# Attention of a post-norm block rebuilt: transposed projections, two-piece scores, heads in row halves

## Chip, cores and metric

One core of a Trainium2 chip runs the program. The metric is device time in microseconds (us) of one execution. The kernel before takes 1507.37 us, median of 3 runs (1506.63 to 1508.64).

## What is computed

The change touches the first third of one layer: attention over 8 sequences of 512 rows, width 256, 16 heads of 16. What follows it (first layer norm, router, shared and routed experts, second norm) is the same in both kernels.

```python
def _L0_attn_ref(x, Wqkv, Wo):            # x (8, 512, 256), H = 16, DH = 16
    qkv = (x @ Wqkv).reshape(b, l, 3, H, DH)
    q, k, v = (qkv[:, :, 0], qkv[:, :, 1], qkv[:, :, 2])
    q = q * cos + rotate_half(q) * sin
    k = k * cos + rotate_half(k) * sin
    scores = jnp.einsum('bqhd,bkhd->bhqk', q, k) * DH ** (-0.5)
    attn = jax.nn.softmax(scores, axis=-1)
    out = jnp.einsum('bhqk,bkhd->bqhd', attn, v).reshape(b, l, d)
    return out @ Wo
x = _layernorm(x + _L0_attn_ref(x, L0_attn_Wqkv, L0_attn_Wo), axis=-1)
```

## The kernel before

`attention` works in 32 groups (NG), each of four heads of one sequence. A group has 16 units (U): one unit is one head against one tile of 128 rows. Every engine runs the same hand-written order, `period(p)`, whose step u names what is issued there; semaphores join the engines. For p from -6 to 0 the pipeline fills, a loop runs three passes of eight periods, and the rest is unrolled.

In step u of period p TensorE (PE) issues `score_cols` (L271 to L279: keys by queries into one of two banks psB) for the group p, and `score_rows` (L261 to L269: queries by keys into one of three banks psA) 20 units ahead. VectorE (DVE) takes the row maxima of psA (`row_max`, L470). The maxima are split into three bf16 pieces (`split_max`), turned by 16 small transposes (`turn_max`, L316) and copied into rows 96 to 98 of the query operand, where the column scores subtract them. ScalarE (ACT) takes the exponent of psB (`exps`, L387) into a ring of eight tiles; `add_pv` (L329), once every four steps, multiplies four of them by V in four column strips of the array. ACT copies the sum out (`copy_out`, L399), PE turns it (`turn_out`, L337), DVE divides by the sum of the exponents (`norm_out`, L500 and L510).

Before a head can be scored, q and k are projected row tile by row tile (`project`, L350 to L352, 3 matmuls in fp32r for each half of the width), rotated on DVE (`rope`, L526 to L530) and POOL (L245), split into three bf16 pieces by DVE and POOL in turns (L538, L247, L543, L249, L251), spread over six terms on ACT (`spread`, L414 to L417), turned by 8 transposes a head (`turn_head`, L293) and copied to SBUF (`copy_head`, L394). V is projected in step 12. Each x tile is split by ACT (`x_hi`, L424) and POOL (`x_lo`, L236). SyncE (SP) only loads x, stores the output (L200, L203), zeroes the slot buffer at the start (L191, ten stores) and loads the attention rows back (L595).

## Time and profile before

| | |
|---|---|
| time, median of 3 | 1507.37 us |
| profiled execution: time, span | 1512.29 us, 1510.5 us |
| granted TensorE clock, mean | 0.929 |
| busy: PE, DVE, ACT, POOL | 87%, 69%, 65%, 34% of the span |
| longest group: row maxima, L470 | 512 times, 338.9 us |
| second: exponents, L387 | 512 times, 290.0 us |

A busy share is that of the whole span, so it averages the attention with the expert stages behind it. A row "x512 | 338.9, 682" is a count, the total busy time in us and the mean of one in ns. A row of the timeline begins with the start and the duration, both in us; matmuls are pipelined, so the step from one start to the next is their cost, not the duration. What stands in square brackets or behind the last bar is idle time of the engine and what ended it.

### The profile page before, as it was taken

The numbers are of one execution on the slowest core, as the hardware profiler recorded it, in microseconds if no ns is written. First come the engines' busy times: TensorE is split into PE (matmuls) and PEld (weight loads), VectorE is DVE, ScalarE is ACT, GpSimd is POOL, SyncE is SP. The second block draws the span as 40 slices with busy tenths as digits, with TensorE's granted clock in tenths as the row PEclk, the third lists the DMA queues.
The fourth block names the chain that finished last, engine by engine and source line by source line (L and its number), as shares of the span: only waits on it lengthen the run. The fifth ranks groups of instructions, "written<-read, shape, count | busy, mean of one in ns | idle before, by whom it ended". The sixth has DMA issues, their size and how long they took to land. (4 is left out here: it accounts for less than half of the span.)

```text
span 1510.5 us, 30476 instructions
## 1 busy us (share of the span) xinstructions
PE 1317.0 (87%) x9849; PEld 1007.7 (67%) x9920; DVE 1044.7 (69%) x2129; ACT 979.6 (65%) x2014; POOL 518.4 (34%) x493
## 2 busy tenths in 40 slices
PE   3899999999999999689802989999999999997585
PEld 2544444444444443378702989999999999997485
DVE  3788877887888878387401557777777777775377
ACT  5588878887888888477301437666666666664265
POOL 6222212121222200064574004444444444445542
PEclk7799999999999999998955998999999999998698
DMA  8000010001000003320321006677777667762333
GB/s 335 1 1 29 2 31 1 30 1 31 2 29 2 15 1 112 123 74 18 109 104 70 0 19 233 221 221 237 238 231 239 220 219 236 235 217 63 101 102 95
DMA packets 113899, 160.46 MB, mean 106 GB/s; under 512 B 12928, under 2 KB 95872, under 8 KB 112640
## 3 DMA queue, kind: packets, MB, share of 16 engines
q1 hardware_dynamic: 107648, 142.32, 28.5%
q0 software_dynamic: 6144, 16.79, 3.5%
q8 instruction: 58, 0.95, 0.3%
q14 instruction: 49, 0.40, 0.1%
HBM read 121.86 MB, written 37.22 MB: 105 GB/s over the span
## 5 line engine op out<-in xcount | busy, mean ns | idle before, releaser
L470 DVE TENSOR_REDUCE att_mx<-att_psA 128x1 f32<-128x512 f32 x512 | 338.9, 682 | 62.0 <-PE att_psA L269 59.7
L387 ACT ACTIVATE att_prob<-att_psB 128x512 f32<-128x512 f32 x512 | 290.0, 602 | 81.4 <-PE att_psB L279 69.9
L1465 ACT ACTIVATE exp_psU<-exp_psU,ew_b 128x256 f32<-128x256 f32 x312 | 126.8, 444 | 154.2 <-PE exp_psU L1422 154.2
L269 PE MATMUL att_psA<-att_qk 96*128 96x512 bf16 x512 | 197.8, 388 | 8.9 <-DVE att_mx L470 5.3
L1497 DVE CAST exp_hh<-exp_psU 128x512 fp32r<-128x512 f32 x156 | 107.4, 688 | 110.2 <-ACT exp_psU L1465 110.2
L1420 PE MATMUL exp_psU<-exp_xh,exp_w1h 128*128 128x256 f32 x624 | 177.9, 285 | 2.1 <-DVE exp_w1l L1492 2.1
L1405 PE MATMUL exp_psD<-exp_w2h,exp_hh 128*128 128x256 f32 x624 | 179.6, 288 | 0.0
L1422 PE MATMUL exp_psU<-exp_xh,exp_w1l 128*128 128x256 f32 x624 | 177.5, 285 | 0.0
L1421 PE MATMUL exp_psU<-exp_xl,exp_w1h 128*128 128x256 f32 x624 | 177.5, 284 | 0.0
L279 PE MATMUL att_psB<-att_qk 128*128 128x512 bf16 x441 | 170.2, 387 | 7.8 <-issue 5.3
L1407 PE MATMUL exp_psD<-exp_w2h,exp_hl 128*128 128x256 f32 x624 | 176.5, 283 | 0.0
L1406 PE MATMUL exp_psD<-exp_w2l,exp_hh 128*128 128x256 f32 x624 | 176.5, 283 | 0.0
L1373 POOL TENSOR_TENSOR exp_w2l<-ew_w,exp_w2h 128x512 fp32r<-128x512 f32 x80 | 105.3, 1316 | 139.9 <-ACT exp_w2h L1456 139.9
L1373 POOL TENSOR_TENSOR exp_w2l<-exp_w,exp_w2h 128x512 fp32r<-128x512 f32 x76 | 100.0, 1315 | 125.8 <-ACT exp_w2h L1456 125.8
L329 PE MATMUL att_psV<-att_prob,att_V 128*32 128x512 f32 x1024 | 136.9, 607 | 0.8 <-ACT att_prob L387 0.7
L279 PEld LDWEIGHTS att_psB<-att_qk 128*128 128x128 bf16 x512 | 49.5, 97 | 131.9 <-ACT att_prob L387 93.3
L394 ACT ACTIVATE att_qk<-att_psT 96x1024 bf16<-96x1024 bf16 x128 | 130.5, 1020 | 9.6 <-PE att_psT L293 9.6
L293 PEld LDWEIGHTS att_psT<-att_ident,att_stack 128*96 128x96 bf16 x1024 | 94.5, 127 | 57.5 <-ACT att_qk L394 5.3
L921 ACT ACTIVATE shr_h<-shr_psU,all_sb 128x256 f32<-128x256 f32 x80 | 38.3, 482 | 133.6 <-PE shr_psU L913 49.9
L1420 PEld LDWEIGHTS exp_psU<-exp_xh,exp_w1h 128*128 128x128 f32 x624 | 120.8, 194 | 2.5 <-DVE exp_xl L1488 2.5
L1421 PEld LDWEIGHTS exp_psU<-exp_xl,exp_w1h 128*128 128x128 f32 x624 | 120.7, 193 | 0.0
L1422 PEld LDWEIGHTS exp_psU<-exp_xh,exp_w1l 128*128 128x128 f32 x624 | 120.7, 193 | 0.0
(186 smaller groups left out, 3344.1 us busy)
## 6 DMA issues: line engine op xcount, KB each, us to landing
ew_w<-ew SPq DMA_DIRECT2D x40, 1024.0 KB
exp_w<-ew SPq DMA_DIRECT2D x38, 1024.0 KB, 6.3
exp_xs<-slots_x SPq DMA_DIRECT2D x39, 256.0 KB, 6.1
slots_y<-exp_ys SPq DMA_DIRECT2D x39, 256.0 KB, 6.9
slots_x<-pre_acc SPq DMA_DIRECT2D x9, 1024.0 KB, 14.2
ew_b<-eb SPq DMA_DIRECT2D x39, 128.0 KB, 5.9
att_xt<-xT SPq DMA_DIRECT2D x8, 512.0 KB, 4.6
attn_rows<-att_ob SPq DMA_DIRECT2D x8, 512.0 KB, 3.2
```

What stands on the lines that cost most here:

```text
L269: pe.matmul(psA[A_BANK[n % U]][:, :], r[:, 0, qt * P:(qt + 1) * P], r[:, 1, :], start=True, stop=True).then_inc(s_amm, 1)
L279: pe.matmul(psB[n % 2][:, :], r[:, 1, kt * P:(kt + 1) * P], r[:, 0, :], start=True, stop=True).then_inc(s_bmm, 1)
L329: m = pe.matmul(psV[32 * j:32 * j + 32, :], V[:, b % 2, kt, hg * G + j, :], prob[:, (n + j) % PR, :], start=(kt == 0), stop=(kt == NT - 1))
L387: act.activation(prob[:, n % PR, :], psB[n % 2][:, :], ACT.Exp, scale=SCALE).then_inc(s_exp, 1)
L470: dve.reduce_max(mx[:, g % 2, n % U:n % U + 1], psA[A_BANK[n % U]][:, :], AX_X).then_inc(s_max, 1)
L1373: pool.tensor_tensor(w2_piece(w2l, q), w2_piece(w2[t.k], q), w2_piece(w2h, q).bitcast(F32), ALU.subtract).then_inc(s_w2l, 1)
L1405: pe.matmul(ps, hh[:, h, rows], w2h[:, h, :], start=(h == 0 and r == 0), stop=False, skip_group_check=True)
L1406: pe.matmul(ps, hh[:, h, rows], w2l[:, h, :], start=False, stop=False, skip_group_check=True)
L1407: ins = pe.matmul(ps, hl[:, h, rows], w2h[:, h, :], start=False, stop=(h == HC - 1), skip_group_check=True)
L1420: pe.matmul(ps, w1h[:, c, cols], xh[:, t.k, c, :], start=(c == 0), stop=False)
L1421: pe.matmul(ps, w1h[:, c, cols], xl[:, t.k, c, :], start=False, stop=False)
L1422: ins = pe.matmul(ps, w1l[:, c, cols], xh[:, t.k, c, :], start=False, stop=(c == DC - 1))
```

## The change

- **Projections.** Block i holds q (i even) or k (i odd) of eight heads, already transposed: 128 rows, 512 positions. It is projected twice, once with the columns of the weights as they are and once with the two halves of each head exchanged, so that the rotation needs no exchange. That is 12 matmuls of 512 columns in place of 6, four in each of steps 1 to 3. ACT copies both to SBUF; POOL multiplies by cos and sin, adds (twice, once rounded to fp32r) and subtracts: five operations on 128x512. DVE has no part in it.
- **Stacking.** The pieces (two of fp32r, not three of bf16) are placed by DMA: SP issues 24 transfers a block, each of 16 rows of 2 KB from SBUF to SBUF (three terms, four pairs of heads, two halves). There are 32 blocks. `turn_head`, `copy_head` and `spread` go.
- **Scores.** The operands are fp32r, with 48 rows (50 for the column scores) that start at partition 0 or 64; units alternate between the halves, and rows and columns are ordered so that consecutive matmuls use different halves.
- **Maxima.** Two pieces, one transpose, one copy of 32x128, then one store to a DRAM buffer and, after it has landed, two loads into the query operand. `turn_out` now waits for that copy.
- **Lead and SP.** Row scores run 29 units ahead instead of 20. SP's whole order is written out by period; the slot buffer is zeroed from period 25 on instead of at the start, and all attention rows but the last are loaded behind it.

The diff, cut to its core:

```diff
-    TERMS = 6
-    KR = TERMS * DH
+    PAIRS = P // (2 * DH)
+    HALF = P // 2
+    KQ = 3 * DH
+    KM = KQ + 2
+    NB = 2 * D // P
+    BLOCKS = B * NB
+    SLOTS = 4
+    BOUNCE = 4
...
+    A_LEAD = U + 13
...
-    T_LEAD = A_LEAD + 8
-    PROJECT_QK, ROPE, COPY_OUT, TURN_OUT, NORM_OUT = (1, 2), (2, 3, 4), 4, 8, (8, 9)
-    PROJECT_V, COPY_V, SPLIT_MAX, TURN_MAX, COPY_MAX = 12, 12, 12, (13, 15), (14, U)
-    PIECE_1, PIECE_2, SPREAD, SPLIT_X = 7, 13, 0, 14
+    PROJECT_QK, EVICT_QK = (1, 2, 3), (3, 4)
+    SPLIT_MAX, TURN_MAX, COPY_MAX = 4, 6, 7
+    COPY_OUT, TURN_OUT, NORM_OUT = 5, 8, (10, 11)
+    PROJECT_V, COPY_V, SPLIT_X = 9, 11, 14
...
-    Q_PIECES, K_PIECES = (1, 1, 1, 2, 2, 3), (1, 2, 3, 1, 2, 1)
-    assert len(Q_PIECES) == len(K_PIECES) == TERMS
+    Q_PIECES, K_PIECES = (0, 1, 0), (0, 0, 1)
...
+        hl = a.sb("hl", [P, 2, 2, L], F32R)
+        qs = a.sb("qs", [P, SLOTS, PAIRS, L], F32R)
+        ks = a.sb("ks", [P, SLOTS, PAIRS, L], F32R)
...
+        w = prob[:, :, :].rearrange("p n l -> p (n l)")[:, 0:DC * WN].rearrange("p (c n) -> p c n", c=DC)
+        max_rows = nc.dram_tensor("max_rows", (BOUNCE, 2 * U, P), F32, kind="Internal").ap()
...
+            def stack_block(i):
+                hb, kind = i // 2, i % 2
+                sp.wait_ge(s_lo, i + 1)
+                if hb == 0:
+                    sp.wait_ge(s_ones, 2)
+                if hb >= SLOTS:
+                    sp.wait_ge(s_bmm, 2 * U * (hb - SLOTS + 1))
+                if hb >= 1:
+                    sp.wait_ge(s_stk[kind], STACKED * hb)
+                for half in range(2):
+                    for m, piece in enumerate((Q_PIECES, K_PIECES)[kind]):
+                        rows = slice(half * HALF + m * DH, half * HALF + (m + 1) * DH)
+                        for j in range(PAIRS):
+                            src = half * HALF + j * DH
+                            sp.dma_start((qs, ks)[kind][rows, hb % SLOTS, j, :].bitcast(F32),
+                                         hl[src:src + DH, kind, piece, :].bitcast(F32)).then_inc(s_stk[kind], 16)
+            def place_max(g):
+                sp.wait_ge(s_mev, g + 1)
+                sp.dma_start(max_rows[g % BOUNCE], mrow[:, :].bitcast(F32)).then_inc(s_mout, 16)
+                sp.wait_ge(s_mout, 16 * (g + 1))
+                if g >= 1:
+                    sp.wait_ge(s_min, 32 * g)
+                for half in range(2):
+                    src = max_rows[g % BOUNCE, half * U:(half + 1) * U].rearrange("(m j t) q -> m j (t q)", m=2, t=NT)
+                    dst = qs[half * HALF + KQ:half * HALF + KM, slot_of(g), 2 * (g % 2):2 * (g % 2) + 2, :]
+                    sp.dma_start(dst.bitcast(F32), src).then_inc(s_min, 16)
...
+            for p in range(-QK_LEAD, NG + 1):
+                if p % 4 == 2 and 2 <= (p + 6) // 4 + 2 < B:
+                    b = (p + 6) // 4
+                    sp.wait_ge(s_xl, b + 1)
+                    load_x(b + 2)
+                if p % 4 == 1 and 0 <= (p - 5) // 4 < B:
+                    store_out((p - 5) // 4)
+                if valid(p + 1, NG):
+                    place_max(p + 1)
+                if valid(p + QK_LEAD, BLOCKS):
+                    stack_block(p + QK_LEAD)
+                if p >= TAIL:
+                    sp.wait_ge(s_init, 3)
+                    for c in pieces[2 * (p - TAIL):2 * (p - TAIL) + 2]:
+                        n = min(zero.shape[1], slots.shape[1] - c)
+                        sp.dma_start(slots[:, c:c + n], zero[:, 0:n]).then_inc(s_zero, 16)
+            sp.wait_ge(s_zero, 16 * len(pieces))
+            for b in range(B - 1):
+                if b >= B - 3:
+                    sp.wait_ge(s_ost[b % 2], 16 * (b // 2 + 1))
+                norm.load_attention(sp, attn_out, b)
+            store_out(B - 1)
...
-                wait(pool, it, s_qrd, tile + 1, 1)
-                pool.tensor_tensor(rr[:, :], rc[:, :], rs[:, :], ALU.add).then_inc(s_rr, 1)
-                wait(pool, it, s_p1, tile + 1, 1)
-                pool.tensor_tensor(heads_of(r1), heads_of(rr), st[:, :, 0, :], ALU.subtract).then_inc(s_r1, 1)
-                wait(pool, it, s_p2, tile + 1, 1)
-                pool.tensor_tensor(st[:, 0:H, 5, :], heads_of(r1)[:, 0:H], st[:, 0:H, 4, :], ALU.subtract).then_inc(s_p3, 1)
-                wait(pool, it, s_p3, tile + 1, 1)
-                pool.tensor_tensor(st[:, H:, 2, :], heads_of(r1)[:, H:], st[:, H:, 4, :], ALU.subtract).then_inc(s_qsp, 1)
-                if t == NT - 1 and valid(tile + 1, NT * B):
-                    x_lo(b + 1, it)
+                hi, lo = hl[:, i % 2, 0, :], hl[:, i % 2, 1, :]
+                wait(pool, it, s_cev, i + 1, 1)
+                pool.tensor_tensor(rc[:, :], rc[:, :], cos[:, :], ALU.mult).then_inc(s_rc, 1)
+                wait(pool, it, s_rev, i + 1, 1)
+                pool.tensor_tensor(rs[:, :], rs[:, :], sin[:, :], ALU.mult).then_inc(s_rs, 1)
+                wait(pool, it, s_rc, i + 1, 1)
+                wait(pool, it, s_rs, i + 1, 1)
+                pool.tensor_tensor(rr[:, :], rc[:, :], rs[:, :], ALU.add)
+                v = STACKED * (i // 2)
+                if it is not None:
+                    pool.wait_ge(s_stk[i % 2], v + it * (STACKED * BODY // 2))
+                elif v > 0:
+                    pool.wait_ge(s_stk[i % 2], v)
+                pool.tensor_tensor(hi, rc[:, :], rs[:, :], ALU.add).then_inc(s_hi, 1)
+                wait(pool, it, s_hi, i + 1, 1)
+                pool.tensor_tensor(lo, rr[:, :], hi.bitcast(F32), ALU.subtract).then_inc(s_lo, 1)
...
             def score_rows(n, it):
-                g, h, qt = n // U, n // NT, n % NT
-                if qt == 0:
-                    wait(pe, it, s_tev, h + 1, G)
+                g, m = n // U, n % U
+                pair, qt, half = 2 * (g % 2) + m // 8, m % 8 // 2, m % 2
+                if m == 0 and g % 2 == 0:
+                    for kind in range(2):
+                        wait(pe, it, s_stk[kind], STACKED * (g // 2 + 1), STACKED // 2)
                 back = next(d for d in range(1, U) if A_BANK[(n - d) % U] == A_BANK[n % U])
                 wait(pe, it, s_max, n - back + 1, U)
-                r = qk[0:KR, g % RING, h % G]
-                pe.matmul(psA[A_BANK[n % U]][:, :], r[:, 0, qt * P:(qt + 1) * P], r[:, 1, :], start=True, stop=True).then_inc(s_amm, 1)
+                part, slot = rows_of(half, KQ), slot_of(g)
+                pe.matmul(psA[A_BANK[n % U]][:, :], qs[part, slot, pair, qt * P:(qt + 1) * P], ks[part, slot, pair, :],
+                          start=True, stop=True).then_inc(s_amm, 1)
             def score_cols(n, it):
                 g, u = n // U, n % U
-                kt, j = u // G, u % G
-                if u % 2 == 0 and u < G:
-                    wait(pe, it, s_mev, 2 * g + 1 + u // 2, 2)
+                kt, pair, half = u // G, 2 * (g % 2) + u % G // 2, u % 2
+                if u == 0:
+                    wait(pe, it, s_min, 32 * (g + 1), 32)
                 wait(pe, it, s_exp, n - 1, U)
-                r = qk[:, g % RING, j]
-                pe.matmul(psB[n % 2][:, :], r[:, 1, kt * P:(kt + 1) * P], r[:, 0, :], start=True, stop=True).then_inc(s_bmm, 1)
...
-            def turn_head(h, half, it):
-                g, b = h // G, h // H
-                if half == 0:
-                    wait(pe, it, s_tev, h, G)
-                    if h % H == 0:
-                        wait(pe, it, s_stk, NT * (b + 1), 1)
-                    if it is None and h == 0:
-                        pe.wait_ge(s_init, 8)
-                        pe.wait_ge(s_const, 2)
-                for t in range(NT):
-                    m = pe.transpose(psT[0:KR, half, t * P:(t + 1) * P], stack[:, b % 2, t, half, h % H, :], ident[:, :])
-                if half == 1:
-                    m.then_inc(s_tmm, 1)
...
+                part, slot = rows_of(half, KM), slot_of(g)
+                pe.matmul(psB[n % 2][:, :], ks[part, slot, pair, kt * P:(kt + 1) * P], qs[part, slot, pair, :],
+                          start=True, stop=True).then_inc(s_bmm, 1)
...
+                for n in range(4 * step, 4 * step + 4):
+                    rot, c, term = n // 6, n // 3 % DC, n % 3
+                    if n == 6:
+                        freed(it, s_rev, i, BLOCKS)
+                    cols = slice((2 * t + rot) * P, (2 * t + rot + 1) * P)
+                    weights, rows = ((wh, xh), (wh, xl), (wl, xh))[term]
+                    m = pe.matmul(psX[rot][:, :], weights[:, c, cols], rows[:, x, c, :], start=(n % 6 == 0), stop=(n % 6 == 5))
+                    if n % 6 == 5:
+                        m.then_inc(s_rmm if rot else s_cmm, 1)
...
+                pe.transpose(psX[1][:, 0:P], mm[:, :], identf[:, :]).then_inc(s_mtr, 1)
...
             def period(p, it):
                 for u in range(U):
                     n = p * U + u
+                    if u % 2 == 1 and valid(n + A_LEAD, NG * U):
+                        score_rows(n + A_LEAD, it)
                     if valid(n, NG * U):
                         score_cols(n, it)
-                    if valid(n + A_LEAD, NG * U):
+                    if u % 2 == 0 and valid(n + A_LEAD, NG * U):
                         score_rows(n + A_LEAD, it)
-                    k = n + T_LEAD
-                    if valid(k // 4, NG * G) and k % 4 < 2:
-                        turn_head(k // 4, k % 4, it)
                     if u % G == ADD_PV and valid(n - ADD_PV - G, NG * U):
                         add_pv((n - ADD_PV - G) // U, ((n - ADD_PV - G) % U) // G, it)
-                    if u in TURN_MAX and valid(p + 1, NG):
-                        turn_max(p + 1, TURN_MAX.index(u), it)
+                    if u in PROJECT_QK and valid(p + QK_LEAD, BLOCKS):
+                        project_qk(p + QK_LEAD, PROJECT_QK.index(u), it)
+                    if u == TURN_MAX and valid(p + 1, NG):
...
-            def copy_head(h, it):
-                g = h // G
-                wait(act, it, s_tmm, h + 1, G)
-                act.activation(qk[0:KR, g % RING, h % G, :, :], psT[0:KR, :, :], ACT.Copy).then_inc(s_tev, 1)
+            def evict_qk(i, rot, it):
+                wait(act, it, s_rmm if rot else s_cmm, i + 1, 1)
+                wait(act, it, s_hi, i, 1)
+                act.activation((rs if rot else rc)[:, :], psX[rot][:, :], ACT.Copy).then_inc(s_rev if rot else s_cev, 1)
...
-            def spread(tile, it):
-                b, t = tile // NT, tile % NT
-                q, k = (stack[:, b % 2, t, i].rearrange("p h (m d) -> p h m d", d=DH) for i in range(2))
-                wait(act, it, s_qsp, tile + 1, 1)
-                act.activation(q[:, :, 1:3, :], q[:, :, 0:1, :].to_broadcast([P, H, 2, DH]), ACT.Copy)
-                act.activation(k[:, :, 3:6:2, :], k[:, :, 0:1, :].to_broadcast([P, H, 2, DH]), ACT.Copy)
-                act.activation(q[:, :, 3, :], q[:, :, 4, :], ACT.Copy)
-                act.activation(k[:, :, 1, :], k[:, :, 4, :], ACT.Copy).then_inc(s_stk, 1)
...
+            def split_max(g, it):
+                m = mx[:, g % 2, :].rearrange("p (h c) -> p h c", h=2)
+                pieces = mm[:, 0:2 * U].rearrange("p (h m c) -> p m h c", h=2, m=2)
+                wait(dve, it, s_max, U * (g + 1), U)
+                wait(dve, it, s_mtr, g, 1)
+                if it is None and g == 0:
+                    dve.wait_ge(s_init, 4)
+                link(dve.tensor_scalar(pieces[:, 0].bitcast(F32R), m, -1.0, None, ALU.mult))
+                linked(it)
+                dve.scalar_tensor_tensor(pieces[:, 1].bitcast(F32R), m, -1.0, pieces[:, 0], ALU.mult, ALU.subtract).then_inc(s_msp, 1)
+            def copy_max(g, it):
+                wait(dve, it, s_mtr, g + 1, 1)
+                wait(dve, it, s_mout, 16 * g, 16)
+                dve.tensor_copy(mrow[:, :], psX[1][0:2 * U, 0:P]).then_inc(s_mev, 1)
...
+    d = np.arange(DH)
+    order = []
+    for first in range(0, D // DH, P // DH):
+        heads = first + np.concatenate([np.arange(0, P // DH, 2), np.arange(1, P // DH, 2)])
+        for part in range(2):
+            for within in (d, (d + DH // 2) % DH):
+                order.append((part * D + heads[:, None] * DH + within[None, :]).ravel())
```

## Rows read from the trace of the kernel before

**Rows 1.** First and last start of the exponents and of the last division.
```profile
L387 ACT ACTIVATE att_prob<-att_psB x512: 582/597/644, 64.8 to 620.4; 128x512 f32<-128x512 f32 x171
...
L510 DVE TENSOR_TENSOR att_ob<-att_psX,att_rden x32: 404/407/424, 91.7 to 623.9; 128x256 f32<-128x256 f32 x32
```

**Rows 2.** Windows: length; busy of PE, PEld, DVE, ACT, POOL; clock; DMA; GB/s.
```profile
44.00:65.00 21.00, 17.73 (x98) 11.21 (x99) 16.38 (x32) 8.58 (x13) 6.24 (x7) 0.69 0.00 1
92.00:576.00 484.00, 467.04 (x3408) 228.68 (x3462) 393.90 (x779) 402.46 (x704) 105.69 (x104) 0.99 0.05 15
402.46:419.90 17.44, 17.23 (x128) 8.41 (x128) 14.65 (x31) 14.70 (x26) 3.77 (x4) 1.00 0.01 1
575.73:591.68 15.95, 14.95 (x116) 6.70 (x116) 12.78 (x24) 13.01 (x21) 0.00 (x0) 1.00 0.66 213
596.17:599.27 3.10, 3.06 (x18) 0.69 (x17) 2.49 (x5) 3.07 (x6) 0.00 (x0) 1.00 0.00 0
616.12:619.01 2.89, 2.32 (x14) 0.47 (x13) 0.00 (x0) 2.17 (x5) 0.00 (x0) 1.00 0.00 0
604.00:612.00 8.00, 6.01 (x42) 1.91 (x40) 2.90 (x7) 4.91 (x9) 0.00 (x0) 1.00 0.01 2
```

**Rows 3.** Timeline of a quarter of group 30, TensorE.
```profile
596.17 1.06 PE L329 MATMUL att_psV<-att_prob,att_V 128*32 128x512 f32 x8
...
597.16 0.39 PE L279 MATMUL att_psB<-att_qk 128*128 128x512 bf16 x1
...
597.39 0.38 PE L269 MATMUL att_psA<-att_qk 96*128 96x512 bf16 x1
...
598.96 0.38 PE L269 MATMUL att_psA<-att_qk 96*128 96x512 bf16 x1
...
599.27 1.07 PE L329 MATMUL att_psV<-att_prob,att_V 128*32 128x512 f32 x8
```

**Rows 4.** Timeline, two consecutive fp32r matmuls of a projection.
```profile
410.54 0.39 PE L351 MATMUL att_psX<-att_wl,att_xh 128*128 128x512 f32 x1
...
410.77 0.40 PE L352 MATMUL att_psX<-att_wh,att_xl 128*128 128x512 f32 x1
```

**Rows 5.** Groups by line, 200 to 400 us.
```profile
L470 DVE TENSOR_REDUCE att_mx<-att_psA 128x1 f32<-128x512 f32 x173 | 115.1, 681 | 20.3 <-PE att_psA L269 19.6
L387 ACT ACTIVATE att_prob<-att_psB 128x512 f32<-128x512 f32 x174 | 98.7, 602 | 31.9 <-PE att_psB L279 28.7 <-remote 1.9
...
L245 POOL TENSOR_TENSOR att_rr<-att_rc,att_rs 128x512 f32<-128x512 f32 x11 | 13.9, 1268 | 93.1 <-DVE att_rs L530 93.1
...
L399 ACT ACTIVATE att_oT<-att_psV 128x512 f32<-128x512 f32 x11 | 6.6, 599 | 0.0
```

**Rows 6.** Timeline of SP's queue: DMA issues.
```profile
2.25 0.65 SPq L183 DMA_DIRECT2D att_sin<-rope_sin  x1
...
572.27 6.87 SPq L595 DMA_DIRECT2D pre_acc<-attn_rows  x7
...
704.73 0.34 SPq L1023 DMA_DIRECT2D shr_mk<-marks  x1
705.12 0.42 SPq L1024 DMA_DIRECT2D shr_trs<-tri  x1
```

**Rows 7.** DMA issues by line: count, KB each, median us to landing.
```profile
out<-out_o SPq DMA_DIRECT2D x32, 128.0 KB, 1.7
...
ew_b<-eb1c SPq DMA_DIRECT2D x39, 4.0 KB, 4.1
...
shr_trs<-tri SPq DMA_DIRECT2D x1, 64.0 KB, 1.9
```

**Rows 8.** Timeline of the fill: weights split, then matmuls at the lower clock.
```profile
5.01 1.48 ACT L427 ACTIVATE att_wh<-att_w 128x1536 fp32r<-128x1536 f32 x1 [3.00 <-DMA att_w<-Wqkv]
...
10.13 0.63 PE L351 MATMUL att_psX<-att_wl,att_xh 128*128 128x512 f32 x1
...
10.56 0.63 PE L352 MATMUL att_psX<-att_wh,att_xl 128*128 128x512 f32 x1
```

309 lines of the change are left out of this document (111 added, 198 removed).

## The prediction

> **What bounds the kernel now.** I read the windows by stage first, then the groups by line inside the attention, then the timeline of a few periods, and last the queue of SP. Attention runs from the first exponent at 64.8 us to the last division at 623.9 us [rows 1]; the stages behind it are untouched, so the sum is made on that stretch. In it PE is busy 467 of 484 us at a granted clock of 0.99, that is at the upper of its two levels, while DVE has 394 and ACT 402 [rows 2]. One period with all its parts takes 17.44 us, of which PE is busy 17.23, ACT 14.70 and DVE 14.65; a late one without projections takes 15.95 [rows 2]. PE is the bound, with ACT and DVE 16% behind.
>
> Busy time of PE overstates work, so I count its cost by steps from one start to the next. A score matmul of 512 columns costs 0.22 to 0.23 us (597.16 to 597.39), an `add_pv` 1.00 (596.17 to 597.16), the change from scores to `add_pv` (598.96 to 599.27) 0.31, which is 0.09 more than a score [rows 3]; an fp32r matmul of 512 columns costs 0.23 [rows 4], the same as bf16. Two quarters (four steps) near the end show floors. With both scores and one `add_pv` and nothing else a quarter takes 3.10 us (596 to 599) [rows 2], and PE's steps explain 2.9 of it: 8 x 0.23 + 1.00 + 0.09. With column scores and `add_pv` alone it still takes 2.89 (616 to 619) [rows 2], though PE's steps are only 4 x 0.22 + 1.09 = 2.0: here two banks, the exponents and the `add_pv` in the way turn in a loop. That loop is what is late next once PE is relieved.
>
> **The change, part by part.**
>
> *PE.* Gone are 32 transposes of heads (0.23 for four, so about 1.8 us a period; this and the next are my estimates from the score step, a quarter as many columns) and 16 of the maxima (about 1.0, now one, 0.2). Added are 6 projection matmuls, 6 x 0.23 = 1.4. If consecutive scores in different row halves run together, 32 scores cost 16 x 0.23 = 3.7 instead of 7.0. The trace has no row halves. Its nearest row is `add_pv`, four column strips: eight matmuls, two for each strip, finish in 1.06 us [rows 3], though each moves 512 columns of fp32 and one such score step is 0.23 even in the faster types; run one after another they would need at least 1.8. So strips of the array do overlap. Both ends are kept: full overlap and none.
>
> The Trainium skill, "TensorE: Matmul & The Clock Gate", Part 3, says that matmuls in different row groups run at once (about 4 ns between starts); by it the 32 scores cost PE 3.7 us, without it 7. "TensorEngine Tiling (Array Packing)" in the Trainium skill, Key Properties, says on the other hand that a change of tiling mode drains the array; the 0.09 us above agrees with a small drain. By that rule the sum would hold the 0.09 at every change, as it does, and a drain of three times that would make the first quarter longer by about 1 us.
>
> A period by quarters then is: steps 0 to 3, PE: 4 x 0.23 of paired scores + 1.09 + 12 x 0.23 of projection + 6 changes x 0.09 = 5.3, say 5.4. Steps 4 to 7: the loop's 2.89 and a part of the 0.60 us `copy_out` [rows 5] = 3.1. Steps 8 to 11: 0.92 + 1.09 + `turn_out` 0.45 and V 0.7 (estimates from the score step: four fp32 transposes as two of them, six matmuls of half the columns as three) + 4 x 0.09 = 3.5, and a new wait: `turn_out` waits for the copy of the maxima, which stands on DVE behind the row maximum of step 7 (0.68 [rows 5]); PE is there about 0.6 us early, with scores and `add_pv` of this group queued behind it. 4.3 with what the loop adds. Steps 12 to 15: 2.9. Sum 15.7. Each fourth period `x_lo` ends late for the projection (an operation twice as wide as the 1.27 us ones [rows 5], begun after step 14), by my estimate 1.2 us or 0.3 a period. **P = 16.0 us** against 17.44. Without projections: 2.9 + 3.1 + 4.1 + 2.9 = 13.0 against 15.95.
>
> *ACT.* 16 exponents x 0.60, two evictions, one `copy_out` at 0.60 [rows 5], V about 0.4: 11.8 us. *DVE.* 16 x 0.68 [rows 5] + about 1.2 for maxima and division = 12.1. The rotation leaves it; the cost is nothing, since both have 4 us of idle time left. *POOL.* Five operations at 1.27 [rows 5] = 6.4, plus x. It is not late by itself, but its results come about 11 us into the period. All three lie beside PE.
>
> *SP.* This is the new chain. The trace has no transfer from SBUF to SBUF. Plain two-dimensional transfers take 0.34 to 0.42 us of SP and follow each other after 0.39 (704.73 to 705.12); a slower single one took 0.65, and in a row of seven long transfers (512 KB each) they take 0.98 (6.87 for seven) [rows 6]. I take d = 0.40 because these move 32 KB in 16 rows, which is nearest to the small ones. A block costs 24 x 0.40 = 9.6 us of SP. The maxima cost it the store's landing, 1.7 [rows 7], and two issues, with waits about 2.8, plus 0.2 for x and output. So SP has 24d + 3.0 = 12.6 us a period: hidden beside 16.0, with 3.4 us of cover. At most `exps` of the next group wait for the maxima: copied 9.5 us into the period, stored by 11.2, loaded (1.9 to land [rows 7]) by 13.9; cover 2.1 us.
>
> The Trainium skill, "DMA: Bandwidth & Descriptors", Rules for kernel authors, says to coalesce, as under 64 KB one pays mostly overhead. It speaks against this change, whose transfers are of 32 KB; by it the placement would be the bound, which is rival B; no row here is of such a transfer.
>
> *Fill.* The weights are 1280 columns instead of 768, so `wh` starts 1.2 us later than at 5.01 and takes 1.48 x 1.67 [rows 8], `wl` and the x pieces after it are as long, and the first matmul is near 13.0 us; 12 matmuls at the lower clock, 0.43 each [rows 8], with evictions and POOL give the first block at 24.3. SP's order puts five blocks before the first maxima: 24.3 + 120d + 4.7 = 77.0 us to the first exponent, 12 later than 64.8. The slots' ten stores move to periods 25 to 29, where no block is stacked; nothing there waits for them.
>
> *Sum.* Before: 64.8 + 26 x 17.44 + 6 x 15.95 + 10 (rest) = 623.9. After: 77 + 26 x 16.0 + 6 x 13.0 + 10 = 581. That is 43 us less: 1512.3 - 43 = 1469 for the profiled execution, and 1507.4 - 43 = **1464 us** against the median, which lies 4.9 us below the profiled one.
>
> **The rivals.**
>
> *A, the halves don't overlap (the change doesn't do what it says).* Then quarters are 6.5, 3.3, 4.6, 3.1, with x 17.7 us a period and 14.2 without projections: 77 + 460 + 85 + 10 = 632, +8 us, **1515**. For it: no row of halves in the trace, and each matmul has its own semaphore wait. Against it: the strips of `add_pv`.
>
> *B, SP becomes the bound: the side that is slower.* The end is 29 + 120d + 26 (24d + 3.0) + 78 + 10 = 195 + 744d, equal to 623.9 at d = 0.58 us. From there on it decides, 7.4 us for each hundredth. At 0.69 (the slower single issue with its gap [rows 6]) it ends at 708, +84: **1592**. At 0.98 it would be 924, +300. For it: 768 transfers, 24 in a row, and one row near 1 us. Against: the small ones.
>
> *C, the bounce of the maxima is late.* Landing of small loads beside other traffic took 4.1 us [rows 7]. With two more us each way the maxima are there at 17.9 and P is about 17.7 to 17.9 in place of 16.0: +3 us, **1510**. Against: the queue is empty then, as the block before has been placed.
>
> *D, the clock.* With PE less dense it could fall to 1.2 GHz, as in the fill (0.69 granted [rows 2]). PE's 13 us of steps would double: beyond 1700. Against: it was 1.00 where PE was busy 6.0 of 8 us (604 to 612) [rows 2].
>
> *E, a better case.* No wait at `turn_out`, no cost of mode changes: P = 14.6, 75 at the start: -85 us, 1422.
>
> **How the numbers follow.** Chances: forecast 0.50, A 0.18, B 0.17, C 0.07, D 0.02, E 0.06. The range 1415 to 1555 takes in E's side, A, C and B up to d = 0.64 and leaves out about 2 in 10. Faster by over 0.2% (3 us, about what a measurement of this kernel can tell from no change): the forecast, E, and the mild ends of A, B and C: 0.66. Same 0.05, slower 0.29.
>
> **What would show it.** Right: column and row scores of different halves starting within 0.05 us of each other; SP issues 0.40 apart; first exponent near 77 us; periods of 16.0 us; no long wait of the first `score_cols` of a period for the loads of the maxima; clock 1.00. Wrong: scores 0.23 apart (A), periods equal to SP's chain with PE waiting on DMA (B, C). The costliest error would be d, then the overlap.

## The result and the profile after

The changed kernel takes 1705.33 us (median of 4 runs, 1699.0 to 1708.66) against 1508.01 us (median of 4) for the kernel before on the same chip. The ratio is 1.130, with an interval of 1.127 to 1.133: 197 us slower, where 43 us faster was forecast.

The profiled execution took 1708.66 us, its span 1706.8. First the granted clock of the core, then the rows of the page that show PE's busy share and the clock in 40 slices of 42.7 us, in tenths.

```profile
core 0: 1706.8 us, clock 0.839
```

```profile
PE   3469988888978989888699219899999999999496
...
PEclk9557678699699596867798659999999999999698
```

The attention fills slices 4 to 19. PE is busy there for 7 to 9 tenths, and its clock is granted for 5 to 9. The two levels are 2.4 GHz (1.00) and 1.2 GHz (0.50), so a slice that shows 7 (0.70 to 0.79) spent 40 to 60% of its time at the lower one. Before, this stretch stood at 0.99 [rows 2].

The first and last start of the exponents and of the last division answer to [rows 1].

```profile
L422 ACT ACTIVATE att_prob<-att_psB x512: 590/597/630, 115.0 to 816.5; 128x512 f32<-128x512 f32 x171
...
L524 DVE TENSOR_TENSOR att_ob<-att_psX,att_rden x32: 414/415/425, 155.2 to 820.1; 128x256 f32<-128x256 f32 x32
```

The first exponent came at 115.0 instead of 64.8, 50 us later. From there to the last division it took 705.1 us instead of 559.1, 146 more. Behind that both kernels need the same, 886.7 and 886.6 us to the end of the span. So the whole loss is 50 us of fill and 146 us of attention.

The windows answer to [rows 2] (length; busy of PE, PEld, DVE, ACT, POOL; granted clock): the whole stretch, a period at full clock and one at a low clock.

```profile
115.00:820.00 705.00, 615.78 (x2656) 258.15 (x2654) 345.89 (x639) 339.30 (x630) 178.44 (x136) 0.78 0.22 61
...
378.28:397.45 19.17, 16.26 (x87) 7.18 (x87) 11.41 (x23) 10.65 (x22) 6.33 (x6) 1.00 0.18 41
416.62:443.20 26.58, 24.63 (x87) 10.21 (x87) 11.49 (x22) 11.59 (x23) 8.66 (x7) 0.61 0.29 78
```

At full clock a period takes 19.2 us (19.9 where the split of x is late), against 17.44 before and 16.0 in the forecast. Where the clock is 0.61 the same 87 matmuls take 26.6, and most periods lie between the two. The stretch has a mean clock of 0.78, which with two levels means 2 x (1 - 0.78) = 44% of its time at 1.2 GHz. ACT and DVE have 11 to 12 us of work in both, about as forecast. PE's own steps and its short waits (2.9 us of the 19.2 are idle) set the period, with other prices than those of the sum.

The timeline of PE in the period at full clock shows them.

```profile
382.55 0.66 PE L363 MATMUL att_psX<-att_identf,att_oT 128*128 128x128 f32 x4 [0.73 <-DVE att_mrow L507]
383.14 0.49 PE L315 MATMUL att_psA<-att_ks,att_qs 48*128 48x512 f32 x1
383.14 0.49 PE L326 MATMUL att_psB<-att_qs,att_ks 50*128 50x512 f32 x1
383.56 0.39 PE L371 MATMUL att_psX<-att_wh,att_xh 128*128 128x256 f32 x1
...
385.89 0.49 PE L315 MATMUL att_psA<-att_ks,att_qs 48*128 48x512 f32 x1
385.89 0.73 PE L326 MATMUL att_psB<-att_qs,att_ks 50*128 50x512 f32 x2
386.23 0.63 PE L315 MATMUL att_psA<-att_ks,att_qs 48*128 48x512 f32 x2
...
394.38 0.40 PE L348 MATMUL att_psX<-att_xl,att_wh 128*128 128x512 f32 x1
394.70 0.49 PE L315 MATMUL att_psA<-att_ks,att_qs 48*128 48x512 f32 x1
394.71 0.49 PE L326 MATMUL att_psB<-att_qs,att_ks 50*128 50x512 f32 x1
395.13 0.50 PE L348 MATMUL att_psX<-att_xh,att_wl 128*128 128x512 f32 x1
395.47 0.40 PE L348 MATMUL att_psX<-att_xh,att_wh 128*128 128x512 f32 x1
```

Row and column scores of different halves do start together (383.14 both; 394.70 and 394.71). The first pair behind other work costs 0.34 us (385.89 to 386.23), not 0.23, and 0.42 where full-array work follows (383.14 to 383.56). The pair right behind it costs 0.24: the row of 386.23 merges two matmuls, lasts 0.63, and a single such record lasts 0.39, so the second starts at 386.47 (0.23 to 0.24 in each of the 33 such places at full clock). So a pair in fp32r does come at the price of one score, but not the first one. The first projection after a pair takes 0.34 too (395.13 to 395.47) where 0.23 is usual. The step from a projection to a pair is 0.32 (394.38 to 394.70), which is 0.09 more than a projection. The turn of the result (L363) waits.

The queue of SP up to the start of that period, then its stacking issues of the queries (count, then minimum, median and maximum in ns) with their landing time.

```profile
363.36 0.31 SPq L209 DMA_DIRECT2D max_rows<-att_mrow  x1
366.01 0.53 SPq L216 DMA_DIRECT2D att_qs<-max_rows  x2
366.65 15.04 SPq L204 DMA_DIRECT2D att_qs<-att_hl  x24
382.52 0.31 SPq L209 DMA_DIRECT2D max_rows<-att_mrow  x1
```

```profile
L204 SPq DMA_DIRECT2D att_qs<-att_hl x384: 507/589/3048, 32.8 to 694.0; - x192
...
DMA to landing us min/median/max: 1.9/1.9/4.8
```

An issue takes 0.59 us and with its gap 0.63 (15.04 / 24). A block costs SP 15.1 us, and with the maxima 18.3 of the period's 19.2 (363.36 to 381.7). That is above the 16.0 us forecast for the whole period: had PE been as fast as forecast, SP would have held it. Here there is 0.8 us of slack (381.7 to 382.52), so SP runs close beside PE.

What PE waited for between 200 and 650 us (sum, times, longest):

```profile
PE att_psB L326 <- ACT att_prob L422: 18.5, 51, 0.5
PE att_psV L386 <- ACT att_oT L433: 17.8, 20, 0.9
PE att_psX L363 <- DVE att_mrow L507: 12.5, 19, 0.7
```

Three short waits come in most periods: a column score for the exponents, the first `add_pv` of a group for the copy of the last sum, and the turn of the result for the maxima. The list names no wait for a DMA in these 450 us.

Last the fill: VectorE's memset of the ones in the stacked keys (minimum, median and maximum in ns, first and last start), and SP's first stacking.

```profile
L530 DVE MEMSET att_ks<- x2: 6885/6885/6885, 2.5 to 11.1; 32x8192 f32 x2
```

```profile
32.85 15.15 SPq L204 DMA_DIRECT2D att_qs<-att_hl  x24
```

Two memsets of 6.9 us stand on DVE ahead of the low pieces of weights and x, without which nothing can be projected. The first block is stacked from 32.85 us, not 24.3, and five blocks follow each other before the first maxima, stored at 110.6: 15.5 us a block.

### The profile page after: what moved, and what is told of

Read it like the earlier page. It is cut to its first block and busy times, and to the rows that moved or that the text cites. A ratio compares the mean times of both kernels' runs of the same rounds, so it can differ in the third digit from the quotient of the medians.

```text
span 1706.8 us, 28141 instructions
## 1 busy us (share of the span) xinstructions
PE 1415.4 (83%) x8608; PEld 1018.9 (60%) x8608; DVE 950.3 (56%) x1874; ACT 842.5 (49%) x1821; POOL 599.1 (35%) x523
## 5 line engine op out<-in xcount | busy, mean ns | idle before, releaser
L422 ACT ACTIVATE att_prob<-att_psB 128x512 f32<-128x512 f32 x512 | 295.9, 600 | 380.1 <-PE att_psB L326 375.3
L326 PE MATMUL att_psB<-att_qs,att_ks 50*128 50x512 f32 x512 | 265.7, 574 | 52.6 <-ACT att_prob L422 29.8
L315 PE MATMUL att_psA<-att_ks,att_qs 48*128 48x512 f32 x512 | 249.2, 560 | 1.4 <-DVE att_mx L489 1.3
L386 PE MATMUL att_psV<-att_prob,att_V 128*32 128x512 f32 x1024 | 177.5, 773 | 27.3 <-ACT att_oT L433 26.5
L326 PEld LDWEIGHTS att_psB<-att_qs,att_ks 50*128 50x128 f32 x512 | 102.2, 224 | 152.7 <-ACT att_prob L422 107.4
L281 POOL TENSOR_TENSOR att_rc<-att_rc,att_cos 128x512 f32<-128x512 f32 x32 | 40.8, 1276 | 402.7 <-ACT att_rc L428 402.7
L315 PEld LDWEIGHTS att_psA<-att_ks,att_qs 48*128 48x128 f32 x512 | 104.2, 228 | 111.3 <-issue 60.5
L1379 PEld LDWEIGHTS exp_psD<-exp_w2l,exp_hh 128*128 128x128 f32 x624 | 119.7, 192 | 0.0
```

What stands on the lines that cost most here:

```text
L315: pe.matmul(psA[A_BANK[n % U]][:, :], qs[part, slot, pair, qt * P:(qt + 1) * P], ks[part, slot, pair, :], start=True, stop=True).then_inc( ...
L326: pe.matmul(psB[n % 2][:, :], ks[part, slot, pair, kt * P:(kt + 1) * P], qs[part, slot, pair, :], start=True, stop=True).then_inc(s_bmm, 1)
L386: m = pe.matmul(psV[32 * j:32 * j + 32, :], V[:, b % 2, kt, hg * G + j, :], prob[:, (n + j) % PR, :], start=(kt == 0), stop=(kt == NT - 1))
L422: act.activation(prob[:, n % PR, :], psB[n % 2][:, :], ACT.Exp, scale=SCALE).then_inc(s_exp, 1)
L1379: pe.matmul(ps, hh[:, h, rows], w2l[:, h, :], start=False, stop=False, skip_group_check=True)
```

## Experiments

The runs were on several chips. On some (the first four runs, the copy at step 4, and the two behind it) the kernel before takes 1396 us instead of 1507: the stages behind the attention are shorter there (776 us behind the last division of the first run, 887 in the changed kernel). Each ratio is against the kernel before on the same chip. What I compare is the stretch of attention, from the first exponent to the last division (559 us before, 705 after). A mean clock of c in it means 2(1 - c) of its time at 1.2 GHz. Each stretch is from one profiled execution, and the two executions of a version differ by up to 12 us in their time, so differences of stretches under some 10 us are not read. The theories at the outset: (1) the halves, or the idle time they leave, take the clock down; (2) SP's transfers hold the period; (3) the price of a pair and of the visits makes the rest.

**Eight transfers a block.** Second and third term of each head hold other values, so this part of the scores is left out.

```diff
-    STACKED = 2 * 3 * PAIRS * 16
+    STACKED = 2 * PAIRS * 16
...
-                    for m, piece in enumerate((Q_PIECES, K_PIECES)[kind]):
-                        rows = slice(half * HALF + m * DH, half * HALF + (m + 1) * DH)
...
+                    rows = slice(half * HALF, half * HALF + KQ)
+                    for j in range(PAIRS):
+                        sp.dma_start((qs, ks)[kind][rows, hb % SLOTS, j, :].bitcast(F32),
+                                     hl[rows, kind, j // 2, :].bitcast(F32)).then_inc(s_stk[kind], 16)
```

> The changed kernel with 8 transfers of 48 rows a block instead of 24 of 16 rows: the same bytes, a third of the issues (it leaves out the right placement of the pieces, so the scores are of other numbers). If SP's issues set the steady periods, they fall from 19.2 and 26.5 us to PE's own, near 16, and the attention ends about 150 us earlier. If SP is only late in the fill, the first exponent comes at about 65 to 80 us instead of 115 (five blocks at 5 us instead of 15), the periods stay at 19.2 us with the clock up and 26.5 with it down, and the whole gains 35 to 50 us: near 1665.

Measured: ratio 1.120 (1.117 to 1.123). The first exponent came at 88.7 instead of 115.0; the stretch stayed (698 us), its clock too (0.79).

The periods at full clock were still 19.2 us. So SP costs 26 us in the fill and next to nothing behind it, as long as a period takes 19 us or more: the number of transfers is not why the attention is long.

**The halves alone, in the kernel before.** Row scores use rows 0 to 63 of the operands, column scores 64 to 127, so a part of the terms is left out of each.

```diff
-                r = qk[0:KR, g % RING, h % G]
+                r = qk[0:64, g % RING, h % G]
...
-                r = qk[:, g % RING, j]
+                r = qk[64:128, g % RING, j]
```

> The kernel before, with its row scores on rows 0 to 63 only and its column scores on rows 64 to 127 only (it leaves out terms of the scores); nothing else is changed, bf16 and order included. If row halves by themselves bring the clock down, the granted clock of the attention falls from 0.99 to 0.8 or less and the time rises by 50 us or more. If halves only overlap and cost a drain at each change of mode, the clock stays near 1.00 and the time moves by less than 30 us either way, with scores of the two halves starting together.

Measured: ratio 0.984 (0.981 to 0.987), stretch 531 us, periods of 16.4 to 17.2 us, clock 0.99. The timeline of PE at full clock:

```profile
363.29 0.39 PE L279 MATMUL att_psB<-att_qk 64*128 64x512 bf16 x1
363.29 0.39 PE L269 MATMUL att_psA<-att_qk 64*128 64x512 bf16 x1
363.51 0.38 PE L279 MATMUL att_psB<-att_qk 64*128 64x512 bf16 x1
```

Here a pair costs 0.22 us, what one score costs in the kernel before, and the first one is no dearer: bf16 halves are two for one. They bring about 1 us a period and don't take the clock down in this kernel.

**All rows in the changed kernel.** Every score matmul runs over 128 rows, that is over both heads of a pair; the scores of two heads are mixed, and the exponent is scaled down so that it stays finite.

```diff
-                part, slot = rows_of(half, KQ), slot_of(g)
+                part, slot = slice(0, P), slot_of(g)
...
-                part, slot = rows_of(half, KM), slot_of(g)
+                part, slot = slice(0, P), slot_of(g)
...
-                act.activation(prob[:, n % PR, :], psB[n % 2][:, :], ACT.Exp, scale=SCALE)
+                act.activation(prob[:, n % PR, :], psB[n % 2][:, :], ACT.Exp, scale=SCALE / 1024)
...
+            dve.memset(qs[:, :, :, :].bitcast(F32), 0.0).then_inc(s_ones, 1)
```

> The changed kernel with all score matmuls on all 128 rows (sums of two heads, and the exponent scaled down so that it stays finite; the scores are not the right ones): no halves, no change of mode between scores and projections, no overlap. If the halves are what takes PE's clock down, it returns to 0.97 or more and the periods are 17 to 18 us throughout, so that the whole is near 1560 (the fill stays 50 us late). If SP or the waits on ACT and DVE take it down, the clock stays near 0.78 and the periods mix 19 and 26 us as before.

Measured: ratio 1.075 (1.072 to 1.078). The windows are the stretch and a period.

```profile
123.00:725.00 602.00, 545.43 (x2658) 284.44 (x2657) 381.55 (x638) 338.66 (x630) 178.52 (x136) 0.99 0.26 71
```

```profile
362.92:381.80 18.88, 17.52 (x88) 9.44 (x88) 12.79 (x22) 10.65 (x21) 6.32 (x6) 1.00 0.21 47
```

The clock is back at 0.99 and the stretch 103 us shorter (96 against the run with eight transfers, on the same chip). Since periods at full clock are nearly as long as in the changed kernel (18.9 and 19.2), most of this is the cost of the clock: about 95 to 103 of the 146 us. The other 43 are mostly periods of 18.9 us instead of 17.5. And with 32 single matmuls the period isn't longer than with 16 pairs: what the pairs save, the visits and waits take back. This run also shows where the 0.34 us come from:

```profile
370.05 0.50 PE L315 MATMUL att_psA<-att_ks,att_qs 128*128 128x512 f32 x1
370.39 0.62 PE L326 MATMUL att_psB<-att_qs,att_ks 128*128 128x512 f32 x2
...
375.32 0.50 PE L326 MATMUL att_psB<-att_qs,att_ks 128*128 128x512 f32 x1
375.66 0.39 PE L348 MATMUL att_psX<-att_xh,att_wh 128*128 128x512 f32 x1
```

There are no halves here, and still the first score behind `add_pv` takes 0.34 us (370.05 to 370.39), and so does a score that comes late (375.32 to 375.66, with 0.15 us of pause before it). The one behind it takes 0.23 (the merged row of 370.39 lasts 0.62, a single one 0.39). The 0.11 us go with the first fp32r matmul behind a pause or another kind of work, not with the halves.

**Consecutive scores in the same half.**

```diff
-    A_LEAD = U + 13
+    A_LEAD = U + 12
```

> The changed kernel with a lead of 28 units instead of 29, so that consecutive row and column scores use the same row half and can't overlap. If the overlap is worth what was forecast (16 x 0.23 = 3.7 us of PE a period), the periods with the clock up are 20 us or longer and the time rises by 20 us or more. If a pair in different halves costs 0.34 to 0.43 us anyway, as against 0.46, the periods change by less than 1 us. If lower density is what brings the clock down, the clock rises here, as PE is busier, and the time could even fall.

Measured: ratio 1.184 (1.181 to 1.188), stretch 765.5 us.

```profile
115.00:881.00 766.00, 675.19 (x2659) 283.05 (x2655) 346.59 (x641) 339.24 (x630) 178.23 (x136) 0.77 0.20 56
```

```profile
419.74 0.50 PE L326 MATMUL att_psB<-att_qs,att_ks 50*128 50x512 f32 x1
420.08 0.40 PE L315 MATMUL att_psA<-att_ks,att_qs 48*128 48x512 f32 x1
...
424.33 0.50 PE L326 MATMUL att_psB<-att_qs,att_ks 50*128 50x512 f32 x1
424.33 0.73 PE L315 MATMUL att_psA<-att_ks,att_qs 48*128 48x512 f32 x2
```

Periods of 20.7 us at full clock instead of 19.2. But the edit does less than it was meant to. A step that stands alone runs its two scores one after the other (419.74 and 420.08), 0.67 us up to the next work instead of 0.42; where two steps follow each other, scores still start together (424.33). Of the 16 steps of the period from 417.11 to 437.77, six are serial: 6 x 0.25 = 1.5 us, which is the difference. So 1.5 us is what six pairs are worth, not all sixteen. The clock is as low as in the changed kernel, with PE busy for the same share of a period at full clock (17.5 of 20.7 us, and 16.3 of 19.2), so this run says nothing on whether a busier PE would keep the clock.

**Fewer visits.** The twelve projections stand in one step; V, the turn of the result and the division together.

```diff
-    PROJECT_QK, EVICT_QK = (1, 2, 3), (3, 4)
+    PROJECT_QK, EVICT_QK = 2, (3, 4)
...
-    COPY_OUT, TURN_OUT, NORM_OUT = 5, 8, (10, 11)
-    PROJECT_V, COPY_V, SPLIT_X = 9, 11, 14
+    COPY_OUT, TURN_OUT, NORM_OUT = 5, 10, (11, 12)
+    PROJECT_V, COPY_V, SPLIT_X = 10, 11, 14
```

> The changed kernel with its work on TensorE put in another order: the twelve projections of Q and K stand in one step of the period instead of three, and the projection of V, the turn of the result and its division stand together at steps 10 to 12. Nothing is left out. TensorE goes from the halves to full arrays and back 4 times a period instead of about 10, and the turn of the result comes three steps after its copy. Theory 1 (a visit to another mode costs .1 to .2 us on either side, and the turn of the result waits 1.2 us a period): a period at the full clock goes from 19.2 to about 16.5 to 17.5 us, the attention stretch gets 40 to 70 us shorter. Rival (the period is bound by something else at the full clock, for example the handshake of the exponents): it stays at 19.0 to 19.3. On the clock: if what takes it down is the idle time between the pieces of work, the low share of the stretch falls well under 40%; if it is what the halves themselves do, the share stays at 40 to 50%.

Measured: ratio 1.120 (1.115 to 1.126), stretch 680 us, mean clock 0.82. Both expectations of the period missed: the shortest are 20.5 us, and each of them holds a piece at the lower clock (a mean of 0.92 from 368.06 to 388.53 us).

Fewer changes didn't make a shorter period. A run of 12 projections (2.9 us) holds back the column scores, ACT has no exponent to take for 4.0 us, and afterwards PE waits for ACT. The mean clock was 0.82 here, 0.78 in the changed kernel; one run can't tell what of the new order did that.

**The fill.** The memsets of the ones go behind the small pieces, slot by slot, and the maxima are placed ahead of the block.

```diff
-                if valid(p + QK_LEAD, BLOCKS):
-                    stack_block(p + QK_LEAD)
+                if valid(p + QK_LEAD - 1, BLOCKS):
+                    stack_block(p + QK_LEAD - 1)
...
-            for half in range(2):
-                dve.memset(ks[half * HALF + 32:half * HALF + HALF, :, :, :].bitcast(F32), 1.0).then_inc(s_ones, 1)
...
+            for s in range(SLOTS):
+                for half in range(2):
+                    dve.memset(ks[half * HALF + 32:half * HALF + HALF, s, :, :].bitcast(F32), 1.0).then_inc(s_ones, 1)
```

> The changed kernel with two edits of its fill alone: VectorE sets the ones of the stacked keys behind the small pieces of weights and input instead of ahead of them, slot by slot, and the sync engine places a group's maxima ahead of the stacking of the block it used to follow. Nothing is left out. Theory (the first exponent at 115.0 is 13.8 us of memsets on VectorE and one block of stacking of about 15 us too late): the first exponent comes at 85 to 92, the stretch from first exponent to last division keeps its length within 10 us, and the time falls by 20 to 30 us. Rival (the first exponent is bound by the blocks alone, and their order only moves them): the first exponent stays above 105.

Measured: ratio 1.125 (1.120 to 1.130). The first exponent came at 94.8, 20 us sooner and a little later than expected (first stacking at 24.5 us, four blocks of 15.2); the stretch grew by 7 us, its clock was 0.78. So the memset (first stacking 8.3 us sooner) and the fifth block together were the cause of the late start, though they gave 20 us and not the 29 that the theory had counted; 11 us remain in the time.

**The type of the scores.** The score matmuls read the upper two bytes of the same stacked values as bf16; the low part of every piece is left out.

```diff
-                pe.matmul(psA[A_BANK[n % U]][:, :], qs[part, slot, pair, qt * P:(qt + 1) * P], ks[part, slot, pair, :],
+                qb, kb = qs[part, slot, pair, :].bitcast(BF16), ks[part, slot, pair, :].bitcast(BF16)
+                pe.matmul(psA[A_BANK[n % U]][:, :], qb[:, 2 * qt * P + 1:2 * (qt + 1) * P:2], kb[:, 1::2],
```

> The changed kernel with its score matmuls, rows and columns, reading the upper two bytes of the same stacked values as bf16, on the same rows of the same halves, so that the low part of every stacked piece is left out. Rows, columns, order, transfers and waits are those of the changed kernel; only the type of the operands differs. Theory 1 (the four-byte type on half the rows is what takes the clock down): the low share of the stretch falls under 10%, and all periods are near 19. Theory 2 (the half of the rows takes it down, in whichever type; the halves in the kernel before kept it for another reason): the low share stays at 40 to 50%. On the pair: if .34 us for two matmuls is a price of the four-byte type, a pair falls to .23 to .27 us and a period at the full clock to about 17.5 to 18; if it is a price of the halves, both stay.

Measured: ratio 1.089 (1.079 to 1.100), stretch 633 us at a mean clock of 0.86, periods at full clock 18.3 to 18.6 us. The timeline of PE:

```profile
245.47 0.40 PE L316 MATMUL att_psA<-att_ks,att_qs 48*128 48x512 bf16 x1
245.47 0.62 PE L328 MATMUL att_psB<-att_qs,att_ks 50*128 50x512 bf16 x2
245.71 0.39 PE L316 MATMUL att_psA<-att_ks,att_qs 48*128 48x512 bf16 x1
```

The first pair falls from 0.34 to 0.24 us. With the run over all rows, where fp32r has the 0.34 without halves, and the second pairs of the changed kernel at 0.24, the 0.34 is a price of the first fp32r matmul behind other work, which neither side of the expectation had; in bf16 it is absent. About ten of the 16 steps of a period begin with such a first score, and 10 x 0.10 fits the 0.6 to 0.9 us that a period gets shorter (1.0 in the run with 64 rows and bf16 below). On the clock both theories fail: 28% of the stretch is at the lower level, neither under 10 nor over 40.

**All 64 rows of a half.** The added rows are ones on the key side and, but for rows 48 and 49 of a half, zeros on the query side. Those two hold zeros for the first eight groups only. From then on the row scores find in them the maxima that were placed in the same slot eight groups earlier, so what is taken as a maximum is shifted by them. The division takes such a shift out again, but the subtraction no longer guards the exponent by the row's own maximum. This also holds for the versions below that keep the 64 rows.

```diff
-                part, slot = rows_of(half, KQ), slot_of(g)
+                part, slot = rows_of(half, HALF), slot_of(g)
...
-                part, slot = rows_of(half, KM), slot_of(g)
+                part, slot = rows_of(half, HALF), slot_of(g)
...
+            dve.memset(qs[:, :, :, :].bitcast(F32), 0.0).then_inc(s_ones, 1)
```

> The changed kernel with its score matmuls over all 64 rows of a half instead of 48 (rows) and 50 (columns); the added rows hold zeros on the query side, so the sums are the same. Theory (the share of the array that works decides on the clock): 64 of 128 rows is still half, and the low share falls only a little, from 45% to perhaps 25 to 40%. Rival (any row count under a full half is what takes the clock down): the share falls under 10%. The length of a period at the full clock stays at 19.2 by both; the first exponent moves to about 123 by the memset of the queries, as with all 128 rows.

Measured: ratio 1.098 (1.089 to 1.107), stretch 629 us.

```profile
124.00:753.00 629.00, 526.66 (x2658) 225.69 (x2656) 344.49 (x638) 338.10 (x630) 178.21 (x136) 0.94 0.25 68
```

The best single edit that leaves nothing out, and one that adds no time to a matmul: periods at full clock stay at 19.2, with PE busy for 16.2 us in them as in the changed kernel (16.3). Only the number of rows differs, and the stretch is 76 us shorter by way of the clock; of these runs this is the clearest evidence that the rows count. The time at the lower level, 13%, is less than the theory's 25 and more than the rival's 10. The memset of the queries, ahead of the first projection here, makes the fill 9 us longer (124.4).

**Both.** 64 rows and bf16; again the low part is left out.

> The two edits of the runs before joined: the score matmuls run over all 64 rows of a half, and read the upper two bytes of the stacked values as bf16 (the low part of every stacked piece is left out). Alone, the rows took the low share of the stretch from 45% to 15%, the type took it to 29%. Theory 1 (rows and type add up, the clock follows how much of the array works and how fast the engine goes on to the next piece of work): the low share falls to 10% or less, the periods at the full clock are 18.2 as with bf16 alone, and the stretch from first exponent to last division comes to 585 to 610 us. Rival (type and rows act through one and the same thing, so that the second brings nothing): the low share stays at 12 to 20% and the stretch at 615 or more. The first exponent is at about 124 by the added memset.

Measured: ratio 1.071 (1.065 to 1.078), stretch 609 us at 0.92, periods of 18.2 to 20.7. The stretch would just do for theory 1, the clock (15% at the lower level) is the rival's: beyond 64 rows the type brings nothing more to the clock, only the cheaper first pair.

**The turn of the result later.**

```diff
-    COPY_OUT, TURN_OUT, NORM_OUT = 5, 8, (10, 11)
+    COPY_OUT, TURN_OUT, NORM_OUT = 5, 10, (11, 12)
```

> The changed kernel with the turn of the result at step 10 instead of 8 of a period, and its division at 11 and 12 instead of 10 and 11. Nothing is left out. Theory 1 (the turn waits about 1.2 us in every period for VectorE's copy of the turned maxima, and that is on TensorE's path): periods at the full clock fall from 19.2 to 18.0 to 18.4 us, the stretch by 20 to 40 us. Rival (behind that wait the exponents are what comes late next, since they run once per column matmul and had waited too): the periods stay at 18.9 to 19.2, and the wait shows up as one for ScalarE. On the clock no theory expects more than 5 points of change in the low share of 45%.

Measured: ratio 1.106 (1.103 to 1.109). Periods at full clock 18.9. The waits of PE, 200 to 650 us, as above:

```profile
PE att_psB L326 <- ACT att_prob L422: 25.8, 80, 0.5
```

The wait for the maxima is gone, and the one for the exponents grew from 18.5 to 25.8 us: of 0.7 us a period, 0.3 were won. That is the rival. Yet the stretch fell by 45 us to 660, mostly since its clock went to 0.86, which neither side had expected. The wait of the first `add_pv` for the copy stayed (0.9 us).

**Combined, with nothing left out:** 64 rows, the later turn, and the fill's edits.

> The changed kernel with what the runs before support, nothing left out: 64 rows in every score matmul, the later turn of the result, the memsets of VectorE behind the weights and slot by slot, and the maxima placed ahead of the stacking. Expected if the parts add up: first exponent at 95 to 103 us, low share of the stretch 10 to 18%, stretch 600 to 625 us, time 1590 to 1615 us on a chip where the kernel before takes 1506, so still slower than it. Rival (the parts get in each other's way, as the clock reacts to every change of order): a stretch of over 640 us.

Measured: ratio 1.078 (1.074 to 1.081), 1624.76 us; first exponent 93.3, stretch 642 us at 0.91. The rival's bound of 640 was just passed, by less than runs of one version differ, and the parts do not add up: the clock, 0.94 with 64 rows alone, is lower with the other parts added. The fill is a little shorter than expected.

**ScalarE's copy at step 4, as in the kernel before,** on top of it.

```diff
-    COPY_OUT, TURN_OUT, NORM_OUT = 5, 10, (11, 12)
+    COPY_OUT, TURN_OUT, NORM_OUT = 4, 10, (11, 12)
```

> The combined kernel of the run before with one more step moved: ScalarE copies the finished sums of a group out at step 4 of the period instead of 5, as the kernel before does. Nothing is left out. In the combined kernel the first quarter of each group waits .9 us for that copy, after the turn's wait is gone. Theory 1 (this wait is on the path that sets the period): periods at the full clock fall from 18.9 to 18.0 to 18.4 us, the stretch from 642 to 610 to 630. Rival, which the later turn already spoke for (what comes late next is always the chain from a column matmul to its exponent to the column matmul two further on, longer by a pair's price than it was): periods stay at 18.7 or more, and the wait for the exponents grows by most of what the wait for the copy loses.

Measured: ratio 1.054 (1.048 to 1.060), the stretch 601.6 us.

```profile
94.00:695.00 601.00, 515.31 (x2656) 222.87 (x2654) 341.07 (x640) 337.39 (x630) 180.18 (x136) 0.96 0.26 72
```

Periods of 18.4 us (18.9 before this edit), theory 1. But some are longer, and here PE does wait for the maxima's loads, 7 times between 200 and 650 us:

```profile
PE att_psB L326 <- DMA att_qs<-max_rows: 6.6, 7, 2.2
```

Two late periods take 23.7 and 23.3 us; SP's queue shows why:

```profile
603.00 1.06 SPq L242 DMA_DIRECT2D slots_x<-pre_acc  x2
604.10 0.90 SPq L209 DMA_DIRECT2D max_rows<-att_mrow  x1
609.79 0.55 SPq L216 DMA_DIRECT2D att_qs<-max_rows  x2
```

The store of the maxima (L209) is issued right behind two large stores that zero the slots, and its landing lets the loads go only 4.8 us after the issue ended, instead of 1.1.

This run was on a chip where the kernel before takes 1396 us and the combined one on a chip where it takes 1508, so two more runs followed, both on a chip where it takes 1397.

> The combined kernel once more, the copy at step 5, on the chip of the run beside it. If the fall of the low share from 20% to 8% came with the moved copy, it is at 17 to 23% here again and the stretch at 635 to 650; if it came from the chip, it is under 12%.

Measured: ratio 1.074 (1.069 to 1.079), stretch 632 us at 0.92. Between the two expectations. The combined kernel is 10 us shorter than on the other kind of chip, no more than runs of one version differ; the moved copy is worth the other 31. Some 15 of these are the 0.5 us in each period at full clock, the rest goes with the clock (0.92 and 0.96).

> The kernel with the copy at step 4, stacked with 8 transfers of 48 rows a block in place of 24 of 16 rows, as in the first run; the second and third term of each head then hold other values than they should, so that part of the computation is left out. In the kernel with the copy at step 4 the sync engine never waited for the maxima to be copied between 200 and 640 us: its own chain (15.1 us of issues, the store's landing, the loads) has taken the place of what TensorE waited for. Theory 1 (by then the queue of SP is the bound, the rival B of the prediction, reached from below): the periods at the full clock fall from 18.4 to 17.2 to 18.0 and the stretch from 602 to 570 to 590. Rival (the chain from column matmul to exponent holds the period at 18.4, SP only runs close beside it): the periods stay at 18.3 to 18.5 and the stretch at 590 to 605. By both the first exponent comes at 65 to 75 us instead of 94.

Measured: ratio 1.023 (1.018 to 1.027). The stretch, a period, and SP's wait from 150 to 600 us:

```profile
74.00:652.00 578.00, 506.32 (x2658) 221.00 (x2656) 341.08 (x642) 337.41 (x630) 178.75 (x136) 0.99 0.24 75
307.98:326.40 18.42, 16.46 (x87) 7.36 (x87) 11.25 (x22) 10.65 (x22) 6.33 (x6) 1.00 0.25 74
```

```profile
SPq L207 <- DVE att_mrow L505: 259.7, 24, 13.6
```

SP now waits 11 us a period, and the typical period stays at 18.4: the rival. But the stretch falls by 24 us, to less than the rival's 590. PE's waits for the maxima (6.6 us) are gone, so with 24 transfers SP did hold up some periods. And 17.5 us are the two late periods, now 14.7 each. From one load of the maxima to the next they took SP 23.5 us (586.29 to 609.79), against 18.0 in an ordinary period (548.49 to 566.50). So of the 8.8 us that each loses, about 5.5 came from the stores that zero the slots, and 3.3 from the 24 transfers themselves: without projections PE needs only 14.7, and SP is the bound there. With 8 transfers SP comes early to the same place, and the maxima are not behind those stores.

```profile
572.74 0.32 SPq L207 DMA_DIRECT2D max_rows<-att_mrow  x1
574.15 0.54 SPq L214 DMA_DIRECT2D att_qs<-max_rows  x2
```

At full clock in nearly all of it, and with part of the scores left out, the rebuilt attention still takes 578 us against 559, with 9 us more of fill.

## Why the prediction was wrong

Against the forecast of 1464 us the kernel is 241 us late. Three terms make this up: the clock, which the sum took as 1.00 (about 95 to 103 us), the period P = 16.0 us at full clock, which is 19.2 (about 100, with the late periods), and the fill (38). The clock is the largest single step that failed, but the period alone would have failed too: at full clock the changed kernel would take about 1602 (1705 - 103), beyond the range's 1555.

**Clock (rival D).** The sum left it at 1.00. Rival D's time, "beyond 1700", came true at a chance of 0.02; by its own working (13 us of steps that double in 26 periods, 338 us more) the time would have been near 1800, and the lower level held for 44% of the stretch only, so that the bound fits is in part luck. The argument was one row: a clock of 1.00 in a window in which PE was busy 6.0 of 8 us (604 to 612) [rows 2]. That window shows bf16 scores over 96 and 128 rows, and it is short. It says nothing of fp32r matmuls over 48 rows. The runs showed clocks of 0.78 with 48 and 50 rows, 0.94 with 64 and 0.99 with 128 (there with single scores instead of pairs), in otherwise the same program; 0.86 with bf16 in place of fp32r; 0.78 to 0.86 with the wait of the turn taken out; and, with 64 rows, 0.92 to 0.96 with the wait for the copy taken out. PE's busy share at full clock doesn't order these runs: it is 0.85 with 48 and with 64 rows, and 0.87 with the later turn. What they have in common, how full the array is and how steadily it is fed, is my reading of them; that the rows count is shown, the rule by which the chip decides was not found.

**Overlap of the halves (rival A, 0.18).** The mechanism is right: both start together, and a pair behind a pair costs 0.24 us, one score. The Trainium skill, "TensorE: Matmul & The Clock Gate", Part 3, says that matmuls in different row groups run at once; the trace agrees (383.14 for both). What the sum lacked is a term that has nothing to do with halves: the first fp32r matmul behind other work takes 0.34 instead of 0.23. The rows that the price was read from could not show it, scores in bf16 and two projections in the middle of a run. The new order has few runs: some ten of its steps and three of its groups of projections begin this way, about 13 x 0.11 = 1.4 us of the 3.2 by which a period exceeds the forecast.

**Mode changes.** 0.09 us each agrees with 0.08 (0.42 against 0.34) and 0.09 (0.32 against 0.23). "TensorEngine Tiling (Array Packing)" in the Trainium skill, Key Properties, says that a change of mode drains the array; the trace agrees in that each change costs these 0.08 to 0.09 us. That the first projection behind a pair takes 0.11 more is the term above.

**The waits.** That of the turn was forecast at 0.6 us and measured at up to 0.73 idle; removing it won 0.3. The forecast's floor for a quarter, the loop of exponents and banks, was the right idea: its wait grew when the turn's was gone. A wait was overlooked, that of the first `add_pv` of a group for the copy that had moved from step 4 to 5, 0.9 us. Taking that copy back won 0.5.

**SP (rival B).** d was 0.40 and is 0.63; the transfers that it was read from are plain ones too, but they are loads from DRAM, and none goes from SBUF to SBUF. The chain of 12.6 us was 18.3, past the 16.0 of the forecast period, and d past the 0.58 from which B was to decide; by B's formula the time would have been about 1547. It didn't decide in the changed kernel, since PE's period was longer still; at 18.4 us a period it held up some of them, and in the late ones it was the bound. "DMA: Bandwidth & Descriptors" in the Trainium skill, Rules for kernel authors, spoke against 32 KB transfers; the trace agrees, at 0.63 us of SP each, but they cost 26 us in the fill, not a bound on every period.

**The bounce of the maxima (rival C)** was hidden in the steady state, PE having no wait for a DMA in its list. The step "nothing there waits for them", of the stores that zero the slots, was wrong: the last blocks are still stacked there, and the maxima's store lands behind those stores. In the kernel with the copy at step 4, whose stacking runs one period later, that cost about 5.5 us in each of two periods. In the changed kernel it happens with one block: the loads go at 727.20, 5.7 us after the store was issued, and PE is idle for 3.6 us before 729.11.

**Fill.** 77.0 was forecast, 115.0 measured. Of these 38 us, 120 x (0.63 - 0.40) = 28 are d, 8.5 (32.85 against 24.3) the memsets, which stand in the diff and were not in the sum, and 2 more that the five blocks took (77.7 us for 75.6). The order of five blocks ahead of the first maxima was seen, and was worth changing.

**ACT, DVE and POOL** were as forecast: 10.65, 11.41 and 6.33 us a period against 11.8, 12.1 and 6.4, all hidden.

## What to carry to other kernels

Where the whole program leans on TensorE's clock, first try a matmul over part of the rows in the existing kernel, or pad it to the full half, and look at the granted clock before anything else. When padding, check what the added rows hold at the time they are read. Price a matmul by its place as well as by its type: the first one behind other work and the ones in a run can differ (0.34 and 0.23 in fp32r). Price a transfer by rows between the same two memories, and where no such row exists, let the range reach to what the chain costs at the worst of them. When a wait is taken out of an engine that is not saturated, what is late next can take part of it back (0.7 became 0.3, 0.9 became 0.5), so plan for the loop behind it.

## What the hardware showed

- The same 87 matmuls take 19.2 us at the granted level of 2.4 GHz and 26.6 where the mean is 0.61, with PE's records busy in 16.3 and 24.6 of them. The level fell in stretches where PE was busy for 7 to 9 tenths.
- Added rows brought the clock up at no cost in the time of a matmul: from 0.78 to 0.94 with 64 in place of 48 and 50 rows, the period at full clock unchanged at 19.2 us.
- A pair of 512 columns in two row halves: 0.22 to 0.24 us in bf16; in fp32r 0.34 behind other work and 0.24 behind another pair. A single fp32r matmul on the full array has the same two prices: 0.34 behind `add_pv` or a pause, 0.23 in a run.
- SP issues a transfer of 16 rows of 2 KB from SBUF to SBUF in 0.59 us (0.63 with the gap), and such a transfer lands after 1.9 us; it issues the store of the maxima to DRAM in 0.31 (363.36), or in 0.90 behind two stores of 1 MB (604.10), and the landing then takes 4.8 us instead of 1.1.
- What stays open: by which measure the clock falls, why the first fp32r matmul is slower, and whether the kernel before with full terms can be brought into two halves. With part of the terms it was 1.6% faster, and it was the only version faster than the kernel before; its six terms and three rows of maxima are 99 rows, which do not fit into 64, and a form that keeps them all was not tried.
